# Last attention of a fused decoder: the score matmuls of two heads and the transposed ones of two older heads issued as one group in four row groups

## What is computed

```python
qh = (q @ Wq + bq).reshape(B, LQ, HEADS, D_K).transpose(0, 2, 1, 3)
kh = (k @ Wk + bk).reshape(B, LKV, HEADS, D_K).transpose(0, 2, 1, 3)
scores = jnp.einsum('bhqd,bhkd->bhqk', qh, kh) * scale
attn = jax.nn.softmax(scores, axis=-1)
out = jnp.einsum('bhqk,bhkd->bhqd', attn, vh)
```

## Time and profile before

| | |
|---|---|
| median of 3 runs | 792.78 us (789.83 to 793.07) |
| the profiled execution's own time | 796.1 us |
| its span | 794.3 us |
| mean granted PE clock | 0.937 |
| PE busy | 719.1 us (91%) |
| DVE, ACT, POOL busy | 489.1, 412.9, 290.0 us |

### The profile page before, as it was taken

The page is one execution under the profiler, slowest core; times in us unless marked ns, Lnnn a source line. Parts: engine busy times, 40 slices in busy tenths (PEclk is TensorE's granted clock), DMA queues, the critical chain, the costliest instruction groups (busy, mean ns, idle before and its releaser), DMA issues.

```text
span 794.3 us, 16402 instructions
## 1 busy us (share of the span) xinstructions
PE 719.1 (91%) x5852; PEld 542.2 (68%) x5852; DVE 489.1 (62%) x1297; ACT 412.9 (52%) x1047; POOL 290.0 (37%) x395
## 2 busy tenths in 40 slices
PE   8788889898897998999999989989888899999886
PEld 6565567575665765899898967758566455767665
DVE  4669777887977885444543455545455658583643
ACT  2234556657566677554544467555562545454311
POOL 0015355565555666110000036423350646363300
PEclk8869989999999999999999999999998756999999
DMA  8537451533727471000000000001011501000000
GB/s 235 126 69 179 123 128 43 122 83 88 161 46 205 112 214 57 2 1 1 1 1 1 1 1 4 1 2 41 4 38 54 185 26 31 2 2 9 8 7 7
DMA packets 25175, 48.11 MB, mean 61 GB/s; under 512 B 7264, under 2 KB 14192, under 8 KB 25096
## 3 DMA queue, kind: packets, MB, share of 16 engines
q1 hardware_dynamic: 24376, 45.66, 22.7%
q10 hardware_dynamic: 720, 1.41, 0.5%
HBM read 17.49 MB, written 0.52 MB: 23 GB/s over the span
## 4 chain that ended last, share of the span: by engine, by line
PE 60%; DVE 14%; issue 10%; ACT 8%; SPq 3%; POOL 2%; DMA 2%; POOLq 0%; ACTq 0%; DVEq 0%
PE SC L839 7%; PE G L550 7%; PE SC L826 7%; PE SC L769 5%; PE G L625 4%; PE SC L861 3%; PE G L938 3%; DVE shift_cols L1542 3%; PE SO L812 3%; ACT causal_probs L1154 2%; PE SO L893 2%; PE SC L743 2%; PE G L647 2%; SPq L1769 1%; PE G L577 1%
## 5 line engine op out<-in xcount | busy, mean ns | idle before, releaser
L1169 ACT ACTIVATE exps<-SC 128x512 f32<-128x512 f32 x192 | 114.4, 597 | 106.8 <-PE SC L769 106.1
L1542 DVE TENSOR_REDUCE shift_cols<-SC 128x2 f32<-128x512 f32 x192 | 129.5, 684 | 32.0 <-PE SC L743 31.5
L1621 POOL TENSOR_TENSOR rstd<-variance,consts 128x2 f32<-128x2 f32 (+1 forms) x48 | 36.8, 766 | 266.0 <-DVE variance L1234 263.0
L1689 POOL TENSOR_TENSOR VB<-exps 128x256 f32<-128x256 f32 x128 | 95.7, 756 | 59.4 <-ACT exps L1169 58.6
L1143 ACT ACTIVATE hidden<-SC,cols 128x256 f32<-128x256 f32 x128 | 53.6, 471 | 65.4 <-PE SC L826 65.3
L1711 POOL TENSOR_TENSOR causal_probs<-causal_probs,inverse 128x256 f32<-128x256 f32 x64 | 51.6, 828 | 68.9 <-DVE inverse L1555 68.9
L1576 DVE SCALAR_TENSOR_TENSOR R<-SC,small,R 128x128 f32<-128x128 f32 x128 | 39.0, 346 | 54.0 <-PE SC L839 53.3
L1154 ACT ACTIVATE causal_probs<-SC,negmax 128x128 f32<-128x128 f32 (+1 forms) x128 | 52.3, 424 | 37.1 <-DVE negmax L1550 37.0
L769 PE MATMUL SC<-stacked_q,stacked_k 100*128 100x256 f32 x256 | 66.9, 344 | 3.5 <-DMA stacked_q<-shift_rows 1.9
L839 PEld LDWEIGHTS SC<-ffn_w,hidden 128*128 128x128 f32 x512 | 66.0, 192 | 5.3 <-issue 1.8
L839 PE MATMUL SC<-ffn_w,hidden 128*128 128x128 f32 x512 | 67.6, 276 | 0.0
(11 more groups left out here) (257 smaller groups left out, 1504.5 us busy)
## 6 DMA issues: line engine op xcount, KB each, us to landing
stacked_k<-k_hi SPq DMA_DIRECT2D x64, 128.0 KB, 2.4
stacked_q<-q_hi SPq DMA_DIRECT2D x64, 128.0 KB, 2.4
ffn_w<-in_ffn_w SPq DMA_DIRECT2D x16, 512.0 KB, 4.8
stacked_k<-k_lo SPq DMA_DIRECT2D x32, 128.0 KB, 2.4
stacked_q<-q_lo SPq DMA_DIRECT2D x32, 128.0 KB, 2.5
packed_k<-U SPq DMA_DIRECT2D x48, 32.0 KB, 1.9
packed_q<-YN SPq DMA_DIRECT2D x48, 32.0 KB, 1.9
a_weights<-in_a_li SPq DMA_DIRECT2D x3, 256.0 KB, 7.4
```

Source lines behind the costliest of these rows:

```text
L1169: fn(exps[:, n % EXPS, :, :].rearrange("p t q -> p (t q)"), SC[1][:, n % 2, :, :].rearrange("p t q -> p (t q)"), ACT.Exp, scale=ATTENTIONS ...
L1542: v.tensor_reduce(shift_cols[:, n // UNIT % 4, :, n % UNIT], SC[0][:, n % 2, :, :], axis=AX.X, op=ALU.max, negate=True).then_inc(head_max, 1)
L1689: v.tensor_tensor(kept[n % EXPS].rearrange("p t q -> p (t q)"), exps[:, n % EXPS, 0, :], exps[:, n % EXPS, 1, :], ALU.add).then_inc(kept_r ...
```

## The change

Only heads of the last attention are treated otherwise. In every even slot the PE now issues, in the front of the slot, one group: for t = 0 the scores of heads n and n + 1 and the transposed scores of heads m and m + 1, where m = n - 10, then the same four for t = 1. The four matmuls of one t lie in four different row groups and go to four different PSUM banks. Odd slots have none. The transposed step lies ten slots behind instead of nine; on ACT and POOL the exponential and the addition move one slot later. DVE's order is unchanged.

```diff
-SHIFT_LAG = 9
+SHIFT_LAG, CROSS_LAG = 9, 10
...
+def late_head(slot, more=0):
+
+    for lag, last in ((SHIFT_LAG, False), (CROSS_LAG, True)):
+        n = head_of(slot - lag - more)
+        if n is not None and (n >= STACK_HEADS) == last:
+            return n
+    return None
...
+                def packed(n, rows):
+                    r, c = slice(HD * (n % UNIT), HD * (n % UNIT) + rows), n // UNIT % 4
+                    return LQ[stream_of(n) % 2][r, c, :], LK[stream_of(n) % 2][r, c, :]
+
+                def cross_products(n, m):
+
+
+                    if n is not None:
+                        if n == STACK_HEADS:
+                            pe.wait_ge(exp_ready, NB * PAIRS)
+                            pe.wait_ge(key_ones_in, 16 * 2)
+                        pe.wait_ge(head_max, n)
+                        if n % UNIT == 0:
+                            pe.wait_ge(packed_in[n // UNIT % 4], 16 * 6 * (stream_of(n) % NB + 1))
+                    if m is not None:
+                        pe.wait_ge(head_exp, m)
+                        if m % UNIT == 0:
+                            pe.wait_ge(shifts_in[m // UNIT % 4], 16 * (m // UNIT // 4 + 1))
+                    for t in range(TT):
+                        of = slice(t * P, (t + 1) * P)
+                        if n is not None:
+                            for h in (n, n + 1):
+                                q, kk = packed(h, HD - 1)
+                                last = mm(SC[0][:, h % 2, t, :], q[:, of], kk, start=True, stop=True)
+                                if t == TT - 1:
+                                    last.then_inc(shift_scores, 1)
+                        if m is not None:
+                            for h in (m, m + 1):
+                                q, kk = packed(h, HD)
+                                last = mm(SC[1][:, h % 2, t, :], kk[:, of], q, start=True, stop=True)
+                                if t == TT - 1:
+                                    last.then_inc(head_scores, 1)
...
                 def front(slot):
-                    if head_of(slot) is not None:
-                        head_products(head_of(slot))
+                    n, m = head_of(slot), late_head(slot)
+                    if n is not None and n < STACK_HEADS:
+                        head_products(n)
+                    even = [h if h is not None and h >= STACK_HEADS and h % 2 == 0 else None for h in (n, m)]
+                    if even != [None, None]:
+                        cross_products(*even)
...
-                    if head_of(slot - SHIFT_LAG) is not None:
-                        head_exponential(head_of(slot - SHIFT_LAG))
+                    if late_head(slot) is not None:
+                        head_exponential(late_head(slot))
...
-                    n = head_of(slot - SHIFT_LAG - 1)
+                    n = late_head(slot, 1)
```

More of the change, by code:

```diff
@@ L723, in head_products @@
                 def head_products(n):
-                    s, U_, k = stream_of(n), n // UNIT, n % UNIT
-                    if n == STACK_HEADS:
-                        pe.wait_ge(exp_ready, NB * PAIRS)
+                    U_, k = n // UNIT, n % UNIT
                     if n >= 2:
@@ L730, in head_products @@
                         wait_emptied(pe, ("k", 0, n))
[L731 to L741, removed]
+                    if k == 0:
+                        pe.wait_ge(stacked[U_ % UNIT_SLOTS], 96 * (U_ // UNIT_SLOTS + 1))
+                    q, kk = SQ[U_ % UNIT_SLOTS][0:3 * HD, k, :], SK[U_ % UNIT_SLOTS][0:3 * HD, k, :]
                     for t in range(TT):
@@ L762, in transposed_products @@
                         wait_emptied(pe, ("q", 0, n))
[L763 to L767, removed]
+                    q, kk = SQ[U_ % UNIT_SLOTS][:, k, :], SK[U_ % UNIT_SLOTS][:, k, :]
                     for t in range(TT):
@@ L986, in back @@
                         unit_values(unit_of(slot, VALUES_AT))
-                    if head_of(slot - SHIFT_LAG) is not None:
-                        transposed_products(head_of(slot - SHIFT_LAG))
+                    n = late_head(slot)
+                    if n is not None and n < STACK_HEADS:
+                        transposed_products(n)
                     if 0 <= slot - M0_AT - UP_LAG < NB * E0:
```

## The result

The change runs in 816.12 us (median of 4, 813.24 to 817.35) beside 792.92 us of the kernel before (four executions each): a ratio of 1.0261 [1.0215, 1.0308]. It is slower, as forecast, and by more than forecast: 801 us was given, and the range ended at 813. A second measurement, in another series, gave 814.94 beside 795.31 us, 1.0221 [1.0153, 1.0289]. The profiled execution took 813.24 us, 17 more than that of before.

A forecast was written before the change was run, and what follows sets the result against it. PE was taken as the bound; waits of 23.8 us less a gain of 15.5 us gave +8.3 us on the 792.8 us of before, so 801 us, range 785 to 813.

The forecast's parts named there:

- The gain: Score matmuls of the last attention: 73 steps become 37 groups, taking 15.5 us of PE time off the path.
- the four don't run together: Rival at the groups: a group costs two steps, no gain, only the waits stay: 817 us; 2%.
- (a): Groups after slots with expert layers wait for an exponential queued behind ACT's Relu: 6.6 us.
- (b): Groups of slots 62 and 46 wait for the second maximum, behind DVE's dispatch tables: 5.2 us.
- (c): Groups of slots 14 and 30 wait for maximum and exponential after the query and key projection: 4.6 us.
- (d): Groups wait where other DVE work, scaling or choice of experts, stands between two maxima: four places, 4.4 us.
- (e): Slots with nothing beside the scores: PE's work is shorter than the chain between groups; eight pairs, 3 us.
- (f): ACT's exponentials and POOL's additions, one slot later, stay hidden ahead of the unit sum: no cost.
- the clock rival: From 677 to 740 us, idle pieces lower PE's clock for a third of the stretch: 13 us more, 814; 11%.
- The rivals of smaller waits: Waits at the groups half of those counted, 787 to 789 us, 22%; or 12 to 19 us, 789 to 797, 19%.
- latencies at the groups: Upper bound on the waits: latencies left out of the terms, some 0.1 us at each of 32 groups.

## Why the prediction was right in its mechanism and too small in its sum

**The gain** was given as 15.5 us and is 15.6, as time in which PE has nothing but score matmuls. That the two agree so well is in part luck. The prediction took 36 steps, 19.0 us, and gave 3.5 of them back for steps that already ran as one. The trace has 20.4 us less cover by score matmuls, and 4.9 us of it were shared with other matmuls before and no longer are. The price of a step and of a group is right. A group costs 0.44 us at the full clock (700.92 to 701.36; 0.45 predicted) and 0.73 at the low one:

```profile
616.62 0.58 PE L768 MATMUL SC<-packed_k,packed_q 31*128 31x256 f32 x2 [1.51 <-ACT exps L1202]
...
617.35 1.22 PE L719 MATMUL G<-CTXT,w_ctx_wk 64*128 64x256 f32 x2
```

By the factor of 3.07 for four row tiles in the Trainium skill ("TensorE: Matmul & The Clock Gate", Measured speedup vs the span model), an estimate for the full clock was 0.57 us. The trace does not agree with that estimate: in this kernel four side by side cost what two do, 0.44 and 0.43 us. The rival by which the four don't run together is refuted by the same rows.

**Terms (a) to (e), waits at the groups**, against what PE's timeline of the change shows: (a) exponential behind the Relu 6.6 predicted, 1.45 + 1.56 + 1.36 + 1.36 + 0.58 + 0.53 = 6.8 measured; (b) maximum behind the dispatch tables: in slot 62 3.5 of idle predicted and 3.52 measured, but in slot 46, taken to be the same, only 1.68; less the 0.7 of before that is 4.5 for 5.2 (the prediction's own numbers, 3.5 for 0.7, make 2.8 a place where its sum took 2.6); (c) projection of queries and keys 4.6, and 2.50 + 2.90 = 5.4, of which more below; (d) other work of DVE 4.4, and 0.98 + 1.02 + 0.75 + 1.58 = 4.3; (e) bare slots 3, and 0.76 + 1.51 + 0.39 + 0.22 = 2.9. The undoing of these waits by reordering, and the making of the loss by strict waits alone, show that they are the cause.

The second wait of (c) hangs on something that the prediction, which read the rows of the first projection, did not name. There the matmuls of the projection end at 644.26, and ACT starts its copy 1.9 us later, released by a DMA that empties the tile it writes to. Before, the same DMA held it for 1.4 us and no group hung on it.

```profile
646.14 0.47 ACT L1145 ACTIVATE U<-G,cols 128x256 fp32r<-128x256 f32 x1 [4.77 <-DMA packed_q<-YN]
```

**The step that failed** is (f): "Exponentials and additions one slot later: hidden", at nothing. With it goes the unwritten assumption that all other work of PE keeps its price. The unit sum waited 4.6 us in place of 1.3 (3.3 more), the expert matmuls 1.4 in place of 0.5 for ACT's copy of `slot_tokens`, and one output projection 0.9 in place of 0.5. Together that is 4.6 us that no term had, and the idle time grew by 28.2 us and not by 23.8. PE's other matmuls cover 104.3 us of the stage where they covered 102.3: 2.0 us more (at least, as 14 of the 128 records of L986 are missing from this trace), with the clock at half in places where it had been full. So PE is busy 13.7 us less and not 15.6, and the stage grows by 23.6 + 4.6 - 13.7 = 14.5 us, where the prediction had 8.3. With the tail's 1.0 this is 15.5.

That the unit sum's wait has its place in the sum is arithmetic, not a verdict on it. With maxima and exponentials early, the additions were worth 7 us. Taken early alone, no gain was seen, and there waits for `shift_rows` and `shift_cols` took 2.4 us back: waits of one in-order stream partly stand in for each other.

**The clock** was a rival at 11%, with 814 us. It came in part: 0.92 from 677 to 740 where there was 1.00, not the third of the stretch at the low level that the rival priced at 13 us. Within the stage, PE's other matmuls take 2.0 us more; what the clock took from the score matmuls is not separated. Over whole executions the mean granted clock of the change is 0.924 (eight executions), that of the kernel before 0.935 to 0.939 in the four series.

**The last part of the gap stays open.** Medians differ by 23 and 20 us; the two profiled executions by 17, of which 15.5 lie in the stage and the tail, and 1.6 in the unchanged part ahead of it. The profiled execution of before was 3.2 us above its median and that of the change 2.9 below, which is 6 of the 23. The unchanged part ends anywhere between 588 and 598 us over all the profiled executions, with no order by kernel. The second profiled execution of the change, 816.63 us, has 4.6 of its 20.5 us over before in that unchanged part. Whether the timed executions of the change have a lower clock in the stage than the two that were profiled, as the one at 0.74 (additions early) suggests, can't be seen: only profiled executions have rows.

**The rivals of smaller waits** (787 to 797, 41% together) fell: waits do not shrink for having followed one another. They did when the order of the queues was changed, which is where such a gain lies.

**The range** ended at 813 and should have reached further. Its upper end stood on the clock rival and on some 3 us of latencies at the groups; no term was added for waits that had not been listed, though only waits at the groups had been looked for.

## What to carry to other kernels

Refilling both halves of a double buffer at one point makes it a single buffer, however well the matmuls pack: count for each refill which producer's queue holds the last result back, and put those results at the front of their slots first, which here was worth 24 us to the packed kernel and 4 to 5 to the unpacked one. Busy time taken off the bounding engine is a gain only as far as the others deliver faster too (here 13.8 us saved, 12.9 of them idle). And where one wait is added, go down the engine's stream behind it: what stands there may wait for results that are now late as well (4.6 us here), and may run at a lower clock.

## What was not expected of the hardware

The clock can fall behind a short wait. After the wait of 3.5 us the granted clock stood at 0.72 over the six microseconds that follow, and the four gather matmuls took 3.52 us for 1.88 before. The expert layer behind a wait of 1.36 us took 1.83, where the one before it took 1.09. Both by stretches, and PE's timeline of the two layers:

```profile
724.00:730.00 6.00, 5.31 (x24) 2.69 (x21) 2.31 (x6) 1.46 (x3) 1.24 (x3) 0.72 0.07 23
...
744.00:750.00 6.00, 5.88 (x49) 5.14 (x53) 0.84 (x2) 1.79 (x6) 1.89 (x3) 0.72 0.00 0
```

```profile
739.17 1.09 PE L986 MATMUL G<-ffn_w,HE 128*64 128x128 f32 x16
...
744.12 0.50 PE L774 MATMUL SC<-packed_q,packed_k 32*128 32x256 f32 x4 [1.36 <-ACT exps L1202]
744.55 1.83 PE L986 MATMUL G<-ffn_w,HE 128*64 128x128 f32 x16
```

Both falls stand at the same two places, again with 0.72 over six microseconds, in the second profile of the change and in that of the change with the additions early. The kernel before has 1.00 at the gather. Other waits of the same length left the clock at full: over the six microseconds behind the 1.56 us at 700.92, and behind another 1.36 us at 732.29, it stood at 1.00. Such a fall is thus not a price to add to each wait, and that the wait makes it is not shown by a run of its own. But it means that the sum of waits can be less than what they cost. The other surprise is that strict waits showed up mainly as PE busy time where no groups were: in the late order 9.1 us busy and 4.0 idle in the stage, in the early one 11.9 and 9.6. In the late order a view of waits alone would have put the stage's growth at a third of what it was.
